# Routing between attention and experts: steps moved from VectorE to GpSimd, with a different set-up order

## What is computed

```
mod = (_silu(L0_c) @ L0_wmod).reshape(L0_c.shape[0], 6, 1, -1)
sa, ca, ga, sb, cb, gb = (mod[:, 0], mod[:, 1], mod[:, 2], mod[:, 3], mod[:, 4], mod[:, 5])
h = _layernorm(x, axis=-1) * (1 + ca) + sa
x = x + ga * _L0_attn_ref(h, ...)
h = _layernorm(x, axis=-1) * (1 + cb) + sb
x = x + gb * _L0_ffn_ref(h, ...)
# in the ffn
logits = jnp.einsum('bsh,eh->bse', x, router_w)
weights, indices = jax.lax.top_k(jax.nn.softmax(logits, axis=-1), 2)
weights = weights / (weights.sum(axis=-1, keepdims=True) + 1e-06)
gate, up = jnp.split(jnp.einsum('bsh,ehi->bsei', x, w13), 2, axis=-1)
y = jnp.einsum('bsei,eih->bseh', jax.nn.silu(gate) * up, w2)
```

## Time and profile before

| | us |
|---|---|
| median of three runs | 1277.39 |
| lowest, highest | 1273.20, 1278.96 |
| the profiled execution, its own time | 1278.54 |
| its span, from first to last instruction | 1276.7 |
| attention block, to the first step of the next | 654.70 |
| from there to the first gather | 33.22 |
| from there to the first expert matmul (701.55) | 13.63 |

### The profile page before, as it was taken

One profiled execution on the slowest core, in us unless ns is written; L12 is line 12 of the kernel. 1 busy time (PEld: TensorE's weight loads), 2 busy tenths in 40 slices (PEclk: granted clock), 3 DMA queues, 4 the chain that ended last, 5 costly groups with the idle time before them and its releaser, 6 DMA issues. The chain is left out here.

```text
span 1276.7 us, 52419 instructions
## 1 busy us (share of the span) xinstructions
PE 1129.7 (88%) x19163; PEld 933.7 (73%) x19163; DVE 898.0 (70%) x2396; ACT 702.4 (55%) x1412; POOL 914.3 (72%) x971
## 2 busy tenths in 40 slices
PE   5899999999999999999513899899999999999994
PEld 1677878788777777787303788787888888887884
DVE  4889999999999999999889444444444444444442
ACT  3668888888888888898533223232322332233231
POOL 3469999999899999999903266666666666666663
PEclk9999999999999999999655899999999999999997
DMA  8333444434334343333374477889878888978862
GB/s 208 77 81 79 121 122 119 120 114 119 98 108 118 92 132 97 112 111 118 96 202 110 88 132 127 130 140 137 151 121 139 144 135 141 137 136 131 135 119 32
DMA packets 214116, 154.14 MB, mean 121 GB/s; under 512 B 113338, under 2 KB 192130, under 8 KB 213746
## 3 DMA queue, kind: packets, MB, share of 16 engines
q1 hardware_dynamic: 171424, 82.51, 26.7%
q0 software_dynamic: 30720, 54.00, 25.5%
q10 hardware_dynamic: 11730, 14.27, 4.6%
HBM read 61.70 MB, written 43.12 MB: 82 GB/s over the span
## 5 line engine op out<-in xcount | busy, mean ns | idle before, releaser
L1483 PE MATMUL psum<-xT,xall 128*128 128x256 f16 x2880 | 329.1, 274 | 21.4 <-issue 19.5
L1585 POOL DMA_INDIRECT out<-late,sidx x135 | 217.4, 1610 | 180.6 <-DVE late L1575 104.0
L1483 PEld LDWEIGHTS psum<-xT,xall 128*128 x2880 | 282.2, 98 | 58.9 <-issue 24.7
L1461 POOL DMA_INDIRECT grow<-moe_rows,gidx x135 | 142.4, 1055 | 87.1 <-DVE gidx L1309 46.3
L1491 ACT ACTIVATE sg<-psum 128x512 f32<-128x512 f32 x120 | 71.4, 595 | 238.8 <-PE psum L1483 193.1
L1496 DVE SCALAR_TENSOR_TENSOR late<-psum,sg 128x512 f32<-128x512 f32 x120 | 82.9, 690 | 157.9 <-ACT sg L1491 108.8
L1560 PE MATMUL psum<-w2s,hT 128*128 x1440 | 168.6, 274 | 3.0 <-DVE w2s L1625 2.7
L1560 PEld LDWEIGHTS psum<-w2s,hT 128*128 128x128 f16 x1440 | 141.6, 98 | 23.7 <-issue 3.5
L781 POOL TENSOR_TENSOR pT<-sc,pT 128x1024 f16<-128x1024 f32 x64 | 136.5, 2134 | 8.0 <-ACT pT L777 8.0
L1507 DVE TENSOR_TENSOR hT<-late,hT 128x512 f16<-128x512 f32 x120 | 83.2, 693 | 83.5 <-ACT hT L1503 76.5
L1503 ACT ACTIVATE hT<-late 128x512 f16<-128x512 f32 x120 | 75.6, 630 | 101.4 <-DVE late L1496 92.8
(11 more groups left out here) (286 smaller groups left out, 2432.3 us busy)
## 6 DMA issues: line engine op xcount, KB each, us to landing
stk<-qk SPq DMA_DIRECT2D x384, 64.0 KB
moe_rows<-hrows SPq DMA_DIRECT2D x64, 256.0 KB, 3.9
out<-xall SPq DMA_DIRECT2D x64, 128.0 KB, 3.4
raw<-in_w ACTq DMA_DIRECT2D x26, 256.0 KB, 3.4
xall<-in_x ACTq DMA_DIRECT2D x24, 256.0 KB, 4.1
raw<-in_w SPq DMA_DIRECT2D x8, 512.0 KB, 8.8
grow<-moe_rows,gidx POOLq DMA_INDIRECT x135
xT<-grow SPq DMA_TRANSPOSE x135
```

Source lines behind the costliest of these rows:

```text
L1461: k.e.indirect_dma_start(grow[:, k.j, q, :], None, rows_dram, at).then_inc(s_g[k.j], 16)
L1483: i = k.e.matmul(bank[:, n * LONG:(n + 1) * LONG], w13s[:, bass.ds(ex_reg * (G * 4 * I) + ((2 * c + b_) * 2 * I + col), P)], xT[:, k.x, a, ...
L1585: k.e.indirect_dma_start(out_rows, bass.IndirectOffsetOnAxis(ap=sidx[:, n:n + 1], axis=0), yo[:, k.v, q, :], None, bounds_check=B * T - 1, ...
```

## The change

The gate weights, the tiles per expert, the slot map and the experts of the slots are formed by GpSimd: 10 steps at the end of the attention block, 76 in the next one, each linked to the one before by a semaphore. What GpSimd hasn't got is written otherwise: a reduction over experts is three additions, a running sum is three shifted additions with copies, a reciprocal is a power with exponent -1, a fused compare-and-add is two steps. The column that TensorE makes for the slot map is copied out by ScalarE. TensorE makes it behind group 8 and not group 3. All eight low halves of w2 come ahead of the first unit's hidden values. In SyncE's queue the single's transposes come one unit sooner. The words of the change also speak of units ordered with the single second; in the code `ORDER` stays as it was.

The set-up changes as well: all three modulation products come at the start, the second shift, scale and both gates are spread in whole banks, two batch pairs at a time, ahead of the first tiles' products; the first scores wait for the gates. The v weights are loaded third in ScalarE's queue, SyncE waits for no weights before its later loads, and GpSimd issues all its nine loads at the start.

```diff
-    def weights(self, e, s_exp, s_chosen, s_weights):
+    def weights(self, e, s_exp, s_chosen):
         e.wait_ge(s_exp, 2)
         e.wait_ge(s_chosen, 1)
-        self.link(e, e.tensor_reduce(self.z, by_token(self.ex), axis=X, op=ALU.add))
-        self.link(e, e.scalar_tensor_tensor(out=self.g, in0=self.z, scalar=EPS_TOP, in1=self.e2, op0=ALU.mult, op1=ALU.add))
-        self.link(e, e.tensor_scalar(self.g, self.g, 1.0, W_SCALE, ALU.add, ALU.mult))
-        self.link(e, e.reciprocal(self.g, self.g))
-        self.link(e, e.tensor_tensor(self.ex, self.ex, self.chosen, ALU.mult))
-        e.tensor_tensor(self.w8, by_token(self.ex), bc(self.g, E), ALU.mult).then_inc(s_weights, 1)
+        some = self.ex[:, 0:E // 2, :]
+        self.link_beside(e, e.tensor_tensor(self.four, some, self.ex[:, E // 2:E, :], ALU.add))
+        self.link_beside(e, e.tensor_tensor(self.four[:, 0:2, :], self.four[:, 0:2, :], self.four[:, 2:4, :], ALU.add))
+        self.link_beside(e, e.tensor_tensor(self.z, self.four[:, 0, :], self.four[:, 1, :], ALU.add))
+        self.link_beside(e, e.tensor_scalar(self.z, self.z, EPS_TOP, None, ALU.mult))
+        self.link_beside(e, e.tensor_tensor(self.g, self.z, self.e2, ALU.add))
+        self.link_beside(e, e.tensor_scalar(self.g, self.g, 1.0, W_SCALE, ALU.add, ALU.mult))
+        self.link_beside(e, e.memset(self.z, -1.0))
+        self.link_beside(e, e.tensor_tensor(self.g, self.g, self.z, ALU.pow))
+        self.link_beside(e, e.tensor_tensor(self.ex, self.ex, self.chosen, ALU.mult))
+        self.link_beside(e, e.tensor_tensor(self.w8, by_token(self.ex), bc(self.g, E), ALU.mult))
...
         engine_program("sync", e)
-            e.wait_ge(e_placed, 2)
+            e.wait_ge(s_beside, WEIGHT_STEPS)
...
             engine_program("gpsimd", e)
+            early.weights(e, e_exp, e_placed)
...
-            if k == 3 * NHOT:
+            if k == 8 * NHOT:
                 e.wait_ge(s_tno, 4)
-                e.wait_ge(s_maps, 1)
+                e.wait_ge(s_slots, 1)
...
     def route_gpsimd(e):
+        def running(out, of):
+            at, spare = of, (run_a[:, :], run_b[:, :], out)
+            for step, to in zip((1, 2, 4), spare):
+                e.tensor_copy(to[:, 0:step], at[:, 0:step])
+                link(e.tensor_tensor(to[:, step:E], at[:, step:E], at[:, 0:E - step], ALU.add))
+                at = to
+        late.weights(e, s_exp, s_chosen)
+        e.wait_ge(s_cnt, 1)
...
+        link(e.tensor_scalar(ex_of[:, :], at, tend[:, 0:1], None, ALU.is_ge))
+        for x_ in range(1, E - 1):
+            link(e.tensor_scalar(past[:, :], at, tend[:, x_:x_ + 1], None, ALU.is_ge))
+            link(e.tensor_tensor(ex_of[:, :], ex_of[:, :], past[:, :], ALU.add))
+        e.wait_ge(s_col, 1)
...
+        e.tensor_copy(ex_i[:, :], ex_of[:, :]).then_inc(s_ex, 1)
         e.wait_ge(s_w8, 16)
...
-            for u in range(NUNITS + NXT + 1):
-                k, single = unit(e, u), unit(e, u - NXT - 1)
+            for u in range(NUNITS + NXT):
+                k, single = unit(e, u), unit(e, u - NXT)
...
                 if group == 0:
-                    w2_low(range(0, 4))
+                    w2_low(range(0, E))
...
-        e.dma_start(wq32[:, :, 2 * D:3 * D], wvT.rearrange("(c p) n -> p c n", p=P)).then_inc(s_wq, 16)
         wmod_part(e, 2)
-        e.wait_ge(s_wq, 48)
...
-        for n, w in enumerate((wqT, wkT)):
+        for n, w in enumerate((wqT, wkT, wvT)):
...
-            set_up_wait(k.e, "vector", "CA23")
+            set_up_wait(k.e, "vector", "GA")
```

More of the change, by code:

```diff
@@ L105, in __init__ @@
         self.placed, self.lt0, self.ids, self.linked, self.links = placed, lt0, tok_id[:, t0:t1], linked, 0
+        self.beside, self.besides = beside, beside_from
     def link(self, e, ins):
@@ L109, in link, with link_beside @@
         e.wait_ge(self.linked, self.links)
+    def link_beside(self, e, ins):
+        self.besides += 1
+        ins.then_inc(self.beside, 1)
+        e.wait_ge(self.beside, self.besides)
     def largest(self, e):
@@ L148, in count @@
             start = self.start
-        e.tensor_tensor(kept, last, start, ALU.subtract)
+        ins = e.tensor_tensor(kept, last, start, ALU.subtract)
+        if s_kept:
+            ins.then_inc(s_kept, 1)
         self.link(e, e.tensor_tensor(self.where, upto, bc(start, self.n), ALU.subtract))
@@ new lines, in vector_gates @@
+        set_up_done(e.tensor_scalar(gate_sign, raw_gates, 0.0, -0.5, ALU.is_ge, ALU.add), "vector", "sign")
+        set_up_wait(e, "vector", "sign")
+        set_up_done(e.tensor_tensor(gates, raw_gates, gate_sign, ALU.mult), "vector", "times")
+        set_up_wait(e, "vector", "times")
+        set_up_done(e.scalar_tensor_tensor(out=gates, in0=gates, scalar=0.125, in1=gate_sign, op0=ALU.max, op1=ALU.mult),
+                    "vector", "gates")
+    def vector_shifts(e):
+        set_up_wait(e, "vector", "gates")
+        set_up_wait(e, "scalar", "hiG")
+        set_up_done(e.tensor_tensor(mod8s[:, 1, sGA::sGB - sGA, :], gates, mod8s[:, 0, sGA::sGB - sGA, :], ALU.subtract),
+                    "vector", "loG")
+        set_up_wait(e, "tensor", "B2")
+        e.tensor_copy(mods[:, mB2, 0:2, :], two(bkD))
+        set_up_done(e.tensor_copy(mods[:, mB2, 2:4, :], two(bkE)), "vector", "B2")
@@ L1119, in early_rest @@
         e.memset(one, 1.0)
-        e.memset(early.seen[:, 0:1], 0.0)
-        early.weights(e, e_exp, e_placed, e_placed)
+        early.link(e, e.memset(early.seen[:, 0:1], 0.0))
         e.wait_ge(e_prefix, 2)
@@ L1256, in route_vector @@
         late.choose(e, s_chosen)
-        late.weights(e, s_exp, s_chosen, s_weights)
-        e.wait_ge(s_prefix, 2)
-        late.count(e, one, bBefore[:, 0:E * NL].rearrange("p (e t) -> p e t", e=E), bTotal[:, 0:E * NL], cnt[:, :])
+        e.wait_ge(s_tables, 2)
+        late.count(e, one, bBefore[:, 0:E * NL].rearrange("p (e t) -> p e t", e=E), bTotal[:, 0:E * NL], cnt[:, :], s_cnt)
         late.place(e, s_asel)
@@ new lines, in route_gpsimd @@
+        link(e.tensor_tensor(end2, tend[:, :], whole, ALU.subtract))
+        link(e.tensor_scalar(single_end[:, :], odd_end[:, :], tend[:, E - 1:E], None, ALU.add))
+        link(e.tensor_tensor(moved[:, :], single_end[:, :], odd[:, :], ALU.subtract))
+        link(e.tensor_tensor(step, moved[:, :], tend[:, :], ALU.subtract))
+        for m in range(3):
+            ins = e.tensor_copy(maps16[:, m, :, :], bc_mid(maps[0:1, m, :], P // E))
+        ins.then_inc(s_slots, 1)
+        at = iota[:, 1, 0:NSLOTS]
@@ new lines, in route_gpsimd @@
+        link(e.tensor_scalar(ex_of[:, :], at, tend[:, 0:1], None, ALU.is_ge))
[3 more added lines that the diff above has]
+        e.wait_ge(s_col, 1)
+        first, whole, step = [tile_col[:, NGRP + m:NGRP + m + 1] for m in range(3)]
+        link(e.tensor_scalar(tile_at[:, :], tile_col[:, 0:NGRP], whole, step, ALU.is_ge, ALU.mult))
@@ new lines, in route_gpsimd @@
+        link(e.tensor_tensor(tile_at[:, :], tile_at[:, :], tile_col[:, 0:NGRP], ALU.add))
+        link(e.tensor_scalar(tile_at[:, :], tile_at[:, :], first, None, ALU.add))
+        for i in range(NGRP):
+            e.tensor_scalar(onto[:, i, :], number[:, 0:NW], tile_at[:, i:i + 1], None,
+                            ALU.is_equal).then_inc(s_slots, 1)
+        link(e.tensor_scalar(past[:, :], at, tend[:, E - 1:E], 1.0 - E, ALU.is_ge, ALU.mult))
+        link(e.tensor_tensor(ex_of[:, :], ex_of[:, :], past[:, :], ALU.add))
@@ L1388, in route_gpsimd @@
+        for x_ in range(0, E - 1):
+            link(e.tensor_scalar(past[:, :], at, single_end[:, x_:x_ + 1], None, ALU.is_ge))
+            link(e.tensor_tensor(ex_of[:, :], ex_of[:, :], past[:, :], ALU.add))
+        e.tensor_copy(ex_i[:, :], ex_of[:, :]).then_inc(s_ex, 1)
         e.wait_ge(s_w8, 16)
```

256 lines of the change are left out of this document (100 added, 156 removed).

## The result

The changed kernel takes **1291.2 us** in the median of 15 runs (1280.9 to 1295.2), the kernel before 1277.7 in 15 runs beside them (1267.6 to 1297.5). The ratio is **1.0101, 95% interval 1.0076 to 1.0125**: slower by 12.9 us, between 9.7 and 16 (the ratio is taken over undisturbed executions alone, so it isn't the quotient of the two medians, which are 13.5 us apart). The forecast was 1286 with a range of 1271 to 1298. The profiled execution of after has a span of 1293.0 us at a mean clock of 0.939, before 1276.7 at 0.952.

What follows compares the result with a forecast made beforehand. It took TensorE to bound the expert block (busy 484 of 500 us) and VectorE's chain the way from the join to the gather; 7.6 + 7 - 2.7 - 8 + 4 = +7.9 on 1278.5 gave 1286 us, range 1271 to 1298.

Steps and rivals of the forecast that it cites:

- Part 1: End of the attention block: early gate weights on GpSimd, with a long power and the store behind it, cost +7.6 us.
- rival (A): GpSimd's power costs nearly the same at any size, early weights only +0.8 us; total 1278 us, chance 0.25.
- Part 2: Late routing in the next block: 76 GpSimd steps in series, plus waits between GpSimd and VectorE, cost +7 us.
- Rival (C): VectorE's comparisons keep GpSimd out until their ring of four groups stops them, start fully crowded; +19, 1297 us, chance 0.09.
- comparisons longer than 0.69 us: Late routing: the expected sign in the profile after, VectorE's comparisons of L1266 lengthened beside GpSimd's steps.
- Part 3: First expert units: all eight low halves of w2 ahead of the first hidden product remove a 2.71 us wait; -2.7 us.
- The cover that I named: Before the first hidden product: VectorE's 5.73 us idle until 707.52 would hide the other four low halves of w2.
- Part 4: Expert block: the single's transposes one turn sooner in SyncE's queue save -8 us of 10.2 us of TensorE waits.
- Rival (D): Units aren't reordered, only SyncE's queue moves; if landing, not issue, is late, the transposes gain nothing; +16, 1294 us, chance 0.08.
- Part 5: Set-up at the start: crowded loads and a later T1 against fewer small spreads and load orders; +4 us, from -2 to +8.
- the crowding: Start of the kernel: GpSimd's nine loads, 1.2 MB at 207 GB/s, alone take 5.9 us beside the other loads.

Runs made afterwards that it cites:

- r2: The changed kernel with the early gate weights back on VectorE; 1.0062 of the kernel before.
- r12: The changed kernel with a product in place of the early gate weights' power (output wrong); 1.0030 of the kernel before.
- r7: The changed kernel with VectorE's sixteen comparisons started only when GpSimd has made the maps; 1.0101 of the kernel before.
- r8: r4 with the late gate weights on GpSimd, all else of the routing on VectorE; 0.9849 of the kernel before.
- r11: r8 with two early gate-weight products over 384 elements also moved to GpSimd; 0.9833 of the kernel before.
- r3: The kernel before with only the late routing moved to GpSimd; 1.0087 of the kernel before.
- r4: The kernel before with only the single's transposes one turn sooner and w2's low halves whole ahead of the first unit; 0.9864 of the kernel before.
- r10: The kernel before with the whole new set-up and nothing else; 1.0114 of the kernel before.
- r5: The changed kernel with SyncE's later loads and GpSimd's nine loads held until the q, k and v weights are there; 1.0070 of the kernel before.
- r6: r5 with the v weights loaded from SyncE's queue again; 1.0062 of the kernel before.
- r9: r6 with GpSimd's nine loads issued in its turn 9, behind its first steps; 1.0013 of the kernel before.

## Why the prediction was right, and where its terms were not

The sign and the range held, with 12.9 us measured against +7.9 forecast. Terms that were too small on both sides partly cancelled: the costs of parts 2 and 5 by 4 and by 7 to 11 us, the gains of parts 3 and 4 together by about 6.5. That the sum came within 5 us is to that extent luck.

**Part 1, +7.6: right in size and in mechanism.** The join grew by 7.1 us in the trace; the runs gave 5.0 (r2) and, for the power alone, 9 (r12), each known to 5. The power took 8.15 us where the slope of two rows (0.566 for one element, 1.03 for four) gave 7.8. With this change's 2.94 us for 16 the price is a straight line, and rival (A), a flat power, is out. The Trainium skill's rule in "SBUF — State Buffer", section "Who interferes with whom", that the instruction that starts first keeps the port to the on-chip memory (SBUF) that both engines share for its whole length, didn't hold here for the power: VectorE's steps with two inputs inside its 8.15 us took 0.56 and 0.36 us, as they do in the kernel before, where GpSimd is idle beside them, and VectorE ended at +9.6 behind GpSimd's attention work, not 8 us later. The measurement decides. Beside GpSimd's ordinary elementwise steps the two engines do hold each other up: GpSimd's steps beside VectorE's comparisons go from 0.20 to 0.65 us (after) and from 0.47 to 1.31 (r7), VectorE's beside GpSimd's products from 0.22 to 0.50 (r8) and from 0.36 to 1.07 (r11).

**Part 2, +7: too small by 4.** The weights (+10.4 for +10.6) were right. The mis-sized terms: 3 us for the two engines holding each other up were 5.7 (the maps take 10.7 us beside the comparisons and 6.3 alone in r7, the first half of the experts' steps 7.9 against 6.6 by its own undisturbed forms); and a GpSimd step with one input and a scalar from SBUF, which I had priced like or below one with two inputs, takes more. It is 0.47 us at 75 elements (taken as 0.35, fifteen steps, 1.8 us) and 0.60 at 135 (taken as 0.47, eight steps, 1.0 us), while the two-input step at 75 elements takes 0.34. (At 75 elements the one compares and the other adds; at 8 elements, where both add or subtract, it is 0.31 against 0.20.) Against that the short steps were 1.4 us cheaper than sized. Rival (C)'s mechanism was right at half its price: the comparisons did hold GpSimd back until their ring stopped them. The prediction's sign for it, comparisons longer than 0.69 us, was the wrong one to look at: GpSimd's steps bore nearly all of it.

**Part 3, -2.7: right for the wait, too small for what came with it.** From the first expert matmul to the third unit 25.6 us became 20.7 (-4.9; r3 against r4 24.9 to 20.6). The wait of 2.71 is what I had priced. Missing was the clock: before, the granted clock was at its lower level from 717.6 to 721.0, the down product behind the wait took 4.37 us, and now it takes 2.78. That isn't so in every execution. The same wait in r3, and in r10, where the stretch took 22.9 us:

```profile
724.93 4.13 PE L1590 MATMUL psum<-w2s,hT 128*128 x24 [2.71 <-DVE w2s L1655]
```

```profile
721.22 2.81 PE L1541 MATMUL psum<-w2s,hT 128*128 x24 [2.71 <-DVE w2s L1606]
```

The cover that I named, VectorE's idle time ahead of 707.52, was there: the eight low halves ended 2.79 us before the first step behind them, and 1.50 us before it in r4, where the gather is as early as before.

**Part 4, -8: right, somewhat small.** The waits fell from 10.2 to 1.2 us. With part 3, r4 gave -17.4 (-22 to -13) where the two terms had -10.7. The two traces have -17.0 from the gather to the end: waits of 2.7 and 9.0, the lower clock behind two of them 1.6 and 1.3, 1.2 ahead of the first expert matmul. The last 1.2 us I leave open. Rival (D) was right that nothing reorders the units and wrong in its price: the issue was what had been late.

**Part 5, +4 (at most +8): this is the step that failed**, with 10.6 to 14.6 measured. I had named the crowding and bounded it by GpSimd's 1.2 MB at the mean rate (5.9 us). But the v weights now share the DMA engines with all that SyncE and GpSimd had been kept from asking for: they landed 19.5 us after their issue, in before 8.5, and 8.6 again in r5, from the same queue and with the others held. With the others held the last of the three was there at 15.3 (r5) and 15.6 (r6), whichever queue asked for the v weights. r5 and r9 hold SyncE's and GpSimd's loads together, so which of the two did more isn't shown; counted from one queue alone the bytes in flight came out too small. And I had put T1 behind the modulation product, whereas it hangs on ScalarE's conversion. The spreads and second scales, for which I had 2 us, cost nothing that the ratios show and perhaps 3 to 6 us by the traces (r9). Nor do the runs say why the attention work ends 15.1 us later when T1 is only 11.2 later; the lower clock up to 59.3 us is a candidate.

## What to carry to other kernels

A wait in front of a load is part of the schedule: before taking one away, add up the bytes that can then be in flight ahead of the transfer that the first tile needs, and look at which engine's queue holds that tile's work behind the wait. Before an operation is moved to the slower engine, ask its price per element from rows of two sizes, and check whether its result ends a stage: ten steps beside the path cost nothing (r8), ten at the end of a block cost 7.1 us, with a store that could only start behind them. A win that is mixed with losses shows only when parts are run alone; here a change of +13 us held two edits of three lines worth -17.

## What the runs showed of the hardware

- GpSimd's power is priced by the element: 0.566, 1.03, 2.94 and 8.15 us for 1, 4, 16 and 48 elements a partition, 0.16 us each. VectorE's reciprocal of the same 48 takes 0.45 (r11).
- During the power of 8.15 us VectorE's two-input steps run at their usual 0.56 and 0.36 us; beside ordinary GpSimd steps VectorE's go from 0.22 to 0.50 (r8), beside VectorE's comparisons GpSimd's from 0.20 to 0.65 (after).
- On GpSimd a step with a scalar read from SBUF costs more than one with a second tensor: 0.47 against 0.34 us at 75 elements, 0.31 against 0.20 at 8 (after, r7).
- An order for a load takes GpSimd 0.57 to 0.96 us of its queue, nine of them, of 8 to 270 KB, 5.5 us (after, r5).
- Behind the same wait of 2.71 us TensorE worked at the lower clock in before and r3 (4.37 and 4.13 us for 24 matmuls) and not in r10 (2.81). Behind waits of 3.68 (before) and 5.21 us (r3) it did, at a price of 1.3 and 2.7 us.
